# A four-layer transformer block on one core: token tiles of the attention stage turned one projection later, low parts of weights in four instructions, two activation splits moved behind the last softmax

## The reference, cut to what matters

```python
x = x + tanh(g_xattn[0]) * attention(layernorm(x), ctx)

def attention(h, ctx):                       # weights 512 x 2048
    q = rms_norm(h @ q_w + q_b, nq_s)        # over all 2048 columns
    k = rms_norm(ctx @ ki_w + ki_b, nki_s)
    v = ctx @ vi_w + vi_b
    p = softmax(q_head @ k_head.T / sqrt(128))
    return (p @ v_head, all heads) @ o_w + o_b
```

## Time and profile before

| | |
|---|---|
| median of 3 runs | 2162.28 us (2158.06 to 2167.98) |
| the profiled execution, its own time | 2160.28 us |
| its span | 2158.5 us |
| first attention, by the trace | from 0 to about 923 us of the span |
| busy: PE, PEld | 1953.0 us (90%), 1641.9 us (76%) |
| busy: DVE, ACT, POOL | 998.5, 837.7, 1099.1 us (46%, 39%, 51%) |
| POOL, low parts of weights (L238) | 65 of 4613 ns, 299.8 us |
| POOL, sums of squares (L262) | 112 of 1300 ns, 145.6 us |
| DVE, low parts of activations (L586) | 64 of 1670 ns on average, 105.1 us |

### The profile page before, as it was taken

How to read it: one execution, slowest core, us unless ns; L and a number is a source line. 1 busy time by engine, 2 the same in 40 slices (tenths; PEclk the granted TensorE clock), 3 DMA queues, 4 the chain that set the end, 5 groups by cost and what they waited for, 6 DMA issues and landing times. The chain is left out here.

```text
span 2158.5 us, 30291 instructions
## 1 busy us (share of the span) xinstructions
PE 1953.0 (90%) x10428; PEld 1641.9 (76%) x10428; DVE 998.5 (46%) x1561; ACT 837.7 (39%) x1594; POOL 1099.1 (51%) x821
## 2 busy tenths in 40 slices
PE   6999999999999999969999599997499986799998
PEld 5888788878887788757887499996377764578886
DVE  3547654765476547533331233334466444583111
ACT  3327333633363335421121122223167876344332
POOL 5765576548754775442116855533534322744332
PEclk9999999999999999969999899998699987899999
DMA  4231333033312331254215555423786564521000
GB/s 143 98 107 51 112 103 127 30 129 106 105 52 95 120 106 70 73 188 161 103 50 210 199 181 168 148 92 106 196 230 173 141 155 147 166 102 55 19 20 20
DMA packets 173917, 251.29 MB, mean 116 GB/s; under 512 B 45088, under 2 KB 69664, under 8 KB 173792
## 3 DMA queue, kind: packets, MB, share of 16 engines
q1 hardware_dynamic: 158704, 205.23, 30.0%
q0 software_dynamic: 9472, 34.09, 4.8%
q10 hardware_dynamic: 5616, 10.23, 1.2%
HBM read 182.92 MB, written 66.58 MB: 116 GB/s over the span
## 5 line engine op out<-in xcount | busy, mean ns | idle before, releaser
L238 POOL TENSOR_TENSOR a_w_hl<-a_w_raw,a_w_hl 128x2048 fp32r<-128x2048 f32 x65 | 299.8, 4613 | 162.0 <-ACT a_w_hl L300 161.9
L413 PE MATMUL a_proj<-a_c_hl,a_w_hl 128*128 128x512 f32 x768 | 184.4, 400 | 22.2 <-DVE a_w_hl L530 20.2
L300 ACT ACTIVATE a_w_hl<-a_w_raw 128x2048 fp32r<-128x2048 f32 x66 | 126.2, 1912 | 161.7 <-PE a_proj L413 106.7
L413 PEld LDWEIGHTS a_proj<-a_c_hl,a_w_hl 128*128 128x128 f32 x768 | 147.0, 193 | 54.9 <-issue 20.2
L487 PE MATMUL a_proj<-a_w_hl,a_a_hl 128*128 128x512 f32 x768 | 179.5, 392 | 3.9 <-DVE a_a_hl L586 3.9
L413 PE MATMUL a_proj<-a_w_hl,a_c_hl 128*128 128x512 f32 x768 | 181.3, 392 | 0.0
L319 ACT ACTIVATE a_sq<-a_proj,a_vecs 128x512 f32<-128x512 f32 x128 | 87.9, 689 | 232.8 <-PE a_proj L413 156.1
L413 PE MATMUL a_proj<-a_a_hl,a_w_hl 128*128 128x512 f32 x768 | 176.4, 390 | 0.0
L487 PEld LDWEIGHTS a_proj<-a_w_hl,a_a_hl 128*128 128x128 f32 x768 | 142.7, 188 | 34.3 <-POOL a_w_hl L238 5.5
L413 PEld LDWEIGHTS a_proj<-a_a_hl,a_w_hl 128*128 128x128 f32 x768 | 143.6, 188 | 29.7
L262 POOL TENSOR_TENSOR a_ssum<-a_ssum,a_sq 128x512 f32<-128x512 f32 x112 | 145.6, 1300 | 39.7 <-ACT a_sq L319 36.1
(11 more groups left out here) (251 smaller groups left out, 3663.2 us busy)
## 6 DMA issues: line engine op xcount, KB each, us to landing
a_w_raw<-in_a_ki_w SPq DMA_DIRECT2D x18, 1024.0 KB, 5.1
a_w_raw<-in_a_vi_w SPq DMA_DIRECT2D x16, 1024.0 KB, 5.1
a_w_raw<-in_a_q_w SPq DMA_DIRECT2D x16, 1024.0 KB, 5.1
a_w_raw<-in_a_o_w SPq DMA_DIRECT2D x16, 1024.0 KB, 5.4
b_gu_raw<-in_b_gate_up POOLq DMA_DIRECT2D x32, 352.0 KB, 3.7
l_sorted_rows<-b_zeros SPq DMA_DIRECT2D x39, 256.0 KB, 3.3
b_hs<-l_sorted_rows SPq DMA_DIRECT2D x39, 256.0 KB, 3.2
l_expert_out<-b_yg ACTq DMA_DIRECT2D x39, 256.0 KB, 3.4
```

The costliest lines, as they stand in the source:

```text
L238: pool.tensor_tensor(w_hl[:, s, 1], w_raw[:, s], f32(w_hl[:, s, 0]), ALU.subtract)\
L300: act.activation(w_hl[:, i % 2, 0], w_raw[:, i % 2], ACT.Copy).then_inc(w_high, 1)
L413: mm = pe.matmul(proj[:, j, :], left, right, start=(k == 0 and n == 0), stop=(k == KC - 1 and n == 2))
```

## The change

Four edits, all in `l0_attention`:

- Tile 0 is turned behind projection 1 instead of projection 0, together with tile 1 (PE, ACT and DVE alike). Tiles 2 and 3 stay where they were. SP's load of tile 2 moves behind the load of the weights of group 3, that of tile 3 behind group 4.
- `w_low` on POOL becomes four instructions of 128 x 512, with one semaphore update behind the last.
- `a_low_part(2)` and `a_low_part(3)` on DVE move from u = 13 and 14 to behind the loop over the units. Those of chunks 0 and 1 stay at u = 11 and 12.
- ACT's high parts (`a_high_part`) stay where they are.

```diff
--- before.py
+++ after.py
@@ -202,8 +202,8 @@
                 load_x(1)
                 for i in range(NW):
                     load_w(NW * t + i + 2, (i + 2) % NW)
-                    if i < 2:
-                        load_x(i + 2)
+                    if 0 < i < 3:
+                        load_x(i + 1)
                     if i == O0 - 1:
                         for j in range(TPB):
                             if j < 2:
@@ -235,8 +235,9 @@
             def w_low(n, i):
                 pool.wait_ge(w_high, n + 1)
                 s = i % 2
-                pool.tensor_tensor(w_hl[:, s, 1], w_raw[:, s], f32(w_hl[:, s, 0]), ALU.subtract)\
-                    .then_inc(w_split, 1)
+                for k in range(KC):
+                    ins = pool.tensor_tensor(w_hl[:, s, 1, k], w_raw[:, s, k], f32(w_hl[:, s, 0, k]), ALU.subtract)
+                ins.then_inc(w_split, 1)
 
             def c_low(n, k):
                 pool.wait_ge(c_high, n + k + 1)
@@ -381,8 +382,9 @@
                         w_high_part(NW // 2 * t + (i + 2) // 2 + 1, i % 2)
                     if O0 <= i < NW - 1:
                         a_high_part(4 * (i - O0) + 7)
-                    if i < TPB:
-                        h_high_part(i)
+                    if 0 < i < TPB:
+                        for j in range(0 if i == 1 else i, i + 1):
+                            h_high_part(j)
                     if i == O0 - 1:
                         attention()
 
@@ -494,8 +496,9 @@
 
                 for i in range(O0 - 1):
                     project(i)
-                    if i < TPB:
-                        turn_h(i)
+                    if 0 < i < TPB:
+                        for j in range(0 if i == 1 else i, i + 1):
+                            turn_h(j)
                     if i == AT["v", 0]:
                         sum_squares(0)
                     if i == AT["q", 0]:
@@ -605,8 +608,10 @@
                             dve.tensor_reduce(den[:, m % 4], probs[:, m % 4], AX.X, ALU.add).then_inc(e_sum, 1)
                             dve.wait_ge(e_sum, NU * t + m + 1)
                             dve.reciprocal(rden[:, m % 4], den[:, m % 4]).then_inc(e_rec, 1)
-                        if EARLY < u <= EARLY + 4:
+                        if EARLY < u <= EARLY + 2:
                             a_low_part(u - EARLY - 1)
+                    for n in (2, 3):
+                        a_low_part(n)
 
                 for i in range(NW):
                     if i < TPB:
@@ -614,8 +619,9 @@
                     if i < O0 - 1:
                         for j in range(4):
                             take(i, j)
-                    if i < TPB:
-                        h_low_part(i)
+                    if 0 < i < TPB:
+                        for j in range(0 if i == 1 else i, i + 1):
+                            h_low_part(j)
                     if i == AT["v", 0]:
                         mean_square(0, rk[:], sc_ps[:, 0, 0:TPB], 1.0)
                         diagonal()
```

## The result

The changed kernel took 2160.74 us (median), the kernel before 2167.88 in the same set of 20 runs each; the ratio is 0.9965, interval 0.9952 to 0.9977, which is 7.6 us of 2168. The forecast was 9.4 us less, the likeliest case. The direction held, and the time lies within the range of 2147 to 2163. It lies above the forecast's own 2150 to 2156 because the kernel before, too, took 5.6 us more in this larger set than in the three runs that the forecast started from; 2162.28 - 7.6 would be 2154.7. Within the sum two terms were too small, the gain at the change of block by 3.1 us and the loss at the second output group by 6.0, and they cancelled in part.

A forecast was written before the change was run, and what follows sets the result against it. PE, busy 90% of the span, bounds the kernel; its waits touched by the change total about 25 us. Terms 8.6 + 4.2 + 1.7 - 5.1 = 9.4 us less, from 2162.28 to 2152.9 us; range 2147 to 2163, own range 2150 to 2156.

The forecast's parts named there:

- gain at the change of block: Between blocks: DVE's bias addition ends 3.45 us earlier, less 0.6 for turning tile 0 later; 8.6 us over three changes.
- loss at the second output group: Output projection: DVE splits step between POOL's four instructions, so PE waits 1.27 us longer a block; 5.1 us lost.
- The addition and its chain: Change of block: last bias addition takes 1 to 1.5 us, not 4.3; store, load, statistics and first copy follow earlier.
- group of 6.60: Four POOL subtractions taking 6.60 us, not 5.02, with DVE instructions between: basis for about 0.5 us per DVE turn.
- Turning tile 0 later: Change of block: four transpositions move behind projection 1; no gain while the wait remains, otherwise 0.6 us paid each time.
- Splits behind the softmax: Softmax tail: moving two activation splits on DVE behind the softmax gains 1.05 us a block, 4.2 us in four blocks.
- End of the stage: Last bias addition ends earlier but POOL ends later, so the next stage starts 1.7 us sooner, once (0 to 3.4).
- Projections: k and q projections: each low part on POOL grows by 0.4 us, hidden in POOL's idle time, so costs nothing.
- rival D: POOL becomes the bound of the projections through longer low parts: 16 us slower, 2178 us; chance 0.07.
- Rival C: POOL's queued next instruction goes first, so the four instructions don't let DVE in: 0.8 us slower, 2163.1 us; chance 0.10.
- A: Rival: the second output group costs nothing, as splits miss the borders or wait themselves: 2147.8 us; chance 0.15.
- B: Rival: at the change of block another wait replaces the shrunken one, half of the 8.6 us remains: 2157.2 us; chance 0.13.

The follow-up runs named there:

- halves: Kernel before, with only the low part of weight group 1 on POOL made in two instructions of half the size: ratio 0.9960 to the kernel before.
- quarters only: Kernel before, with every low part of weights on POOL made in four instructions and nothing else changed: ratio 0.9948 to the kernel before.
- turn put back: Changed kernel, with tile 0 turned behind projection 0 again: ratio 0.9956 to the kernel before.

## Why the prediction was right, and where it was not

*The addition and its chain*: right. 1.00 us for the addition (1.0 to 1.5 named), statistics 3.8 behind it, and halves put it at 2.11.

The Trainium skill says that a DVE instruction with two SBUF inputs and a POOL instruction that reads SBUF share a port pair, and that the one that starts first holds it for its whole instruction while the other is blocked ("SBUF — State Buffer", SBUF: two separate sides). The three lengths of the addition, 4.3, 2.1 and 1.0 with one, two and four instructions, agree. They also answer what that page leaves open here: at a border the waiting DVE instruction went ahead of the queued POOL instruction, each time. A DVE instruction with one SBUF input was not held up: in the kernel before, 12 BATCH_NORM_STATS2 of 128 x 512 ran wholly within a low part of 4.6 us (L238) and took 0.68 to 0.70 us, as the other 52 did. One more ran within the group of 6.60 in the earlier trace rows:

```profile
1500.44 0.70 DVE L2125 BATCH_NORM_STATS2 p_stats<-p_xr 128x6 f32<-128x512 f32 x1
```

*Gain at the change of block*: 8.6 forecast, 11.7 measured. The mechanism was right, the size the net of two misses. The kernel before lost 1.6 us more behind two of its three waits, at the lower clock, which the sum left out (+3.2). And the gap of 0.75 to 1.13 us ahead of projection 0, which I had taken as fixed, went away, so that PE waited 1.3 for the first copy instead of 0.3; as the quarters of group 0 alone showed, this gap and the wait behind it share one chain, and their sum is what counts.

*Turning tile 0 later*: forecast as worth nothing with the wait and 0.6 us dear without it; measured +1.5 us in three changes of block, 0.5 each, and no better than before when made alone. Right.

*Splits behind the softmax*: 4.2 forecast and measured, 1.04 a block; the division at 0.42 less and the unit at 0.61 less were both seen (the turns start 2.4 and 2.2 us apart where it was 2.84).

*Loss at the second output group*: the failed step. 1.27 a block forecast, 2.76 measured, 11.0 in all instead of 5.1. The wait itself grew by 1.16, as the group of 6.60 in the earlier trace rows had said; the other 1.6 is the lower clock behind it, a term that the sum did not have. With one instruction for this group both were gone. The trace of before had two such stretches, each behind a wait of 3 us, and none behind 1.4, so the question whether 2.6 would bring one could have been asked.

*End of the stage*: 1.7 forecast, 2.2 measured; POOL's low part now ends last. *Projections*: 0 forecast, 0 measured within 0.05 us a block; POOL's growth of 0.4 was covered (rival D falls). Rival C fell with the 1.00 and A with the 2.55. B did not come, as no wait appeared behind projection 1 or 2 and the gain there was not halved. But a wait of 1.3 stayed ahead of projection 1: I had placed the chain to the first copy 1 us too early (252.6; it came at 253.84, with PE through projection 0 at 253.23).

That the total came out near the forecast is in part luck. The lower clock was in neither term; it gave 3.2 us back at the change of block and took 6.4 at the output group in the traces of the two kernels. How many waits of 2.5 us it follows differs between kernels that do the same there, two or four of four.

## What to carry to other kernels

Where a short DVE instruction with two inputs in SBUF that begins a chain (store, load, normalise) meets a long POOL instruction with SBUF operands, cut the POOL instruction there and only there: the cut gives DVE its turn, and costs POOL 0.14 us a border and 0.45 to 0.5 for each DVE instruction that steps in, which is a loss wherever PE waits for POOL's result. Cost a wait of PE that grows to 2.5 us or more with the clock behind it, not by its length alone, and read the clock of every stretch behind a long wait before summing. A gap and a wait on the same chain are one term.

## What the runs showed of the hardware

The clock behind PE's waits in this stage: behind waits of up to 1.54 us no stretch at the lower level was seen, 28 waits of 1.37 to 1.41 us ahead of group 13 among them. One was seen behind 8 of 12 waits of 2.5 us (changed kernel 4 of 4, quarters only and turn put back 2 of 4 each), and behind 12 of 15 waits of 2.85 to 4.02 us at the change of block (10 of 12 for tile 0, and 2 of 3 for the first copy where only the turn was moved). No wait between 1.54 and 2.5 us occurred. A stretch was 3.41 us long, in two cases 6.83, and one of 3.41 cost 1.6 us. What decides between waits of equal length stays open: within one execution, blocks that do the same differ by it.

PE's gap at the turn of its loop, 0.75 to 1.30 us, fell to 0.04 to 0.5 whenever group 0's low part was in quarters, and in no kernel otherwise. In those the last splits of DVE end 3.3 us sooner (6.5 us ahead of the end of the output projection, not 3.2). The residual addition (L635) that the row of before names as what ended the gap is not what holds PE: it ends 0.83 us ahead of the last weight load's end in both cases, with the gap of 1.13 and with one of 0.04 (quarters for group 0 only). That PE's instruction list then reaches the end of its loop in time is argued from this, not shown.
